# An attention stage and the three dense layers behind it written as one program, with buffers placed by hand

## The chip, the core and the metric

The kernel runs on one core of one Trainium2 chip. Its time is the device time of one launch in microseconds; the medians below are over three runs, and one further execution was taken with the hardware profiler. The engines are called TensorE (PE in the rows; PEld is its weight load), VectorE (DVE), ScalarE (ACT), GpSimd (POOL) and the sync queue (SP).

## The reference

A token matrix `x` of 2048 rows by 512 goes through four residual blocks, all in float32, with inner products kept near float32 accuracy:

```
x = x + attention0(layernorm(x), ctx)     # 16 heads of 128, keys of 128 rows, q and k RMS-normalised
x = x + ffn0(layernorm(x))                # relu(x W1 + b1), relu(. W2 + b2), . W3 + b3 ; 512-1024-1024-512
x = x + attention1(layernorm(x), ctx)     # 32 heads of 16, rotary positions
x = x + experts_and_mlp(layernorm(x))     # gated MLP 2048 wide and a product-key expert lookup
```

The change concerns the first two: in `attention0` every tile of 128 rows attends to its own 128 context rows, heads 0 to 7 and 8 to 15 being independent until their outputs are added.

## The kernel before

Each block is a stage with its own semaphores and its own buffers; `stage_ends()` clears the semaphores and makes all engines wait for one another, and the next stage starts from nothing. Data go between stages through `x1`, `x2`, `x3` in HBM. Within a stage each engine has a list of instructions written out by hand, and semaphores order them across engines; there is no planner.

A float32 product is made of three: each operand is split into a high part (ScalarE, an activation `Copy` that rounds) and a low part (a subtraction, raw minus high), and `product` (L37) adds high by high, high by low and low by high.

`l0_attention` runs 32 steps: steps 0 to 15 do heads 0 to 7 for the 16 row tiles, steps 16 to 31 do heads 8 to 15. Step `s` holds the keys, queries, scores and softmax of tile `s` and, woven in, the end of tile `s-1` (`output`, `turn_p`, `mix`); step 32 is the drain, with only that end. Steps 3 to 13 and 18 to 29 are loops, all others are written out. A step splits its heads in two groups `g` of four. `xres` keeps all rows; `add_y` adds a tile's output there, and `store` writes it to `x1` in the second half. The weights of the first half of the heads are loaded at the start; those of the second half go to `stage` buffers, and around steps 15 and 16 are split into the homes of the first: high parts by ScalarE (L164), low parts by GpSimd (`split_lo(pool, ..., 1)`, L168). In the first half the layer norm's statistics are made on VectorE (L558, L559) and their root on GpSimd (`root`, L274 and L276). `statistics(0)` waits for three loads of `x`, though it reads the first only.

`l0_ffn` runs four chunks of 512 rows. Per chunk: 8 tiles of the first hidden layer (`hidden1`, 12 matmuls each), 8 of the second (`hidden2`, 24 each), and behind each of these a share of the output (`output`, 12 matmuls), with the next chunk's rows normalised, transposed (`turn_x`, L817) and split between. A hidden tile leaves its bank through ScalarE's relu for the high part (L880) and VectorE's relu and subtraction for the low (L938, L941); three banks take turns. Weights come as 16 pieces of 1024 elements a partition through two `stage` buffers: GpSimd fetches and makes the low parts (L799), ScalarE the high ones (L886), in the order W1, W2, W3. The layer norm is wholly on VectorE, its root by ten small instructions (L44 to L48). `hidden2`'s first tile waits for all eight low parts of the first layer.

Of the kernel before, what the change touches and what calls it, by code (L numbers as in the profile page):

```python
# [22 lines left out]
AHEAD = (slice(0, 2), slice(2, NB))  # L23

# [42 lines left out]
def l0_attention(nc, sb, sem, bank, ident, ident_in, x, ctxT, wq, wk, wv, wo, gq, gk, x1):  # L67
# [6 lines left out]


# [58 lines left out]
    LAST_USE = {"wq0": "q_made0", "wq1": "q_made1", "wk0": "k_made0", "wk1": "k_made1", "wv0": "v_made0", "wv1": "v_made1",  # L134
# [25 lines left out]
    def split_hi(act, n, h):  # L160
        act.wait_ge(S[f"{load_of(n)}_staged"], 16 * (h + 1))
        if h:
            act.wait_ge(*at(LAST_USE[n], NB - 1))
        act.activation(home(n, 0), staged(n, h), ACT.Copy).then_inc(S[f"{n}_hi"], 1)  # L164
# [11 lines left out]
    FIRST, LOOP0, END0, LOOP1, END1, LAST = -1, 3, NB - 2, NB + 2, STEPS - 2, STEPS + 1  # L176
# [13 lines left out]
    block = nc.Block()  # L190
    with block:
        @block.sync
        def _(sp):
            x_tiles = x.rearrange("(b p) d -> p b d", p=P)

            def load_res(i):
                tiles = PIECES_OF_X[i]
                sp.dma_start(xres[:, tiles, :], x_tiles[:, tiles, :]).then_inc(S[f"xres_loaded{i}"], 16)

            def load_x(s):  # L200
                row = sp.snap((s - NB) * P)
                if not (isinstance(s, int) and s == NB):
                    sp.wait_ge(*at("xn_ready", s - 1))
                sp.dma_start(x_in[:], x[bass.ds(row, P), :]).then_inc(S["x_loaded"], 16)

            def load_ctx(s):
                if there(s - 1):
                    sp.wait_ge(*at("ctx_split", s - 1))
                row = sp.snap(((s + NB) % NB) * P)
                sp.dma_start(ctx_in[:], ctxT[:, :, bass.ds(row, P)]).then_inc(S["ctx_loaded"], 16)  # L210

            def store(s):
                row, col = sp.snap((s - NB) * P), sp.snap((s - NB) * DM)
                sp.wait_ge(S["y_added"], s + 1)
                sp.dma_start(x1[bass.ds(row, P), :], xres[:].rearrange("p b d -> p (b d)")[:, bass.ds(col, DM)]).then_inc(S["stored"], 16)

            def step(s, second_half=True, storing=True):
                now = s if isinstance(s, int) else None
                if now == FIRST:
                    load_res(0)  # L220
                    load_ctx(0)
                    sp.dma_start(ident[:], ident_in).then_inc(S["ident_loaded"], 16)
                    load_res(1)
                    sp.dma_start(gqk[:, 0:1], gq).then_inc(S["g_loaded"], 16)
                    sp.dma_start(gqk[:, 1:2], gk).then_inc(S["g_loaded"], 16)
                    load_res(2)
                if second_half and there(s + 2):
                    load_x(s + 2)
                if storing:
                    store(s - 1)  # L230
                if there(s + 2):
                    load_ctx(s + 2)
                if now == 0:
                    for i, n in ((3, "wq1"), (4, "wo0"), (5, "wo1")):
                        sp.wait_ge(S[f"{n}_cut"], 1)
                        load_res(i)

            for s in range(FIRST, LOOP0):
                step(s, second_half=False, storing=False)
            with sp.Fori(LOOP0, END0) as s:  # L240
                step(s, second_half=False, storing=False)
            for s in range(END0, LOOP1):
                step(s, storing=s > NB)
            with sp.Fori(LOOP1, END1) as s:
                step(s)
            for s in range(END1, LAST):
                step(s)
            sp.wait_ge(S["stored"], 16 * NB)

        @block.gpsimd  # L250
        def _(pool):
            def fetch(n, h, after=()):
                q, k, v, o = (w[h].rearrange("(k p) w -> p k w", p=P) for w in (wq, wk, wv, wo))
                src = {"wq0": q[:, :, 0:G * D], "wq1": q[:, :, G * D:W], "wv": v, "wk": k, "wo0": o[:, 0:G], "wo1": o[:, G:2 * G]}[n]
                for piece, times in after:
                    pool.wait_ge(S[f"{piece}_cut"], times)
                pool.dma_start(LANDS[h][n].rearrange("p (k w) -> p k w", k=src.shape[1]), src).then_inc(S[f"{n}_staged"], 16)

            def split_ctx(s):
                pool.wait_ge(*at("ctx_hi", s))  # L260
                pool.tensor_tensor(ctxp[1][:], ctx_in[:], ctxp[0][:], ALU.subtract).then_inc(S["ctx_split"], 1)
# [16 lines left out]
            def step(s, roots=False):  # L278
                now = s if isinstance(s, int) else None
                if now == FIRST:  # L280
                    for n in ("wq0", "wk", "wq1", "wv", "wo0", "wo1"):
                        fetch(n, 0)
# [6 lines left out]
                if there(s):  # L289
                    means(s, 0)  # L290
# [1839 lines left out]
```

## Time and profile before

| | us |
|---|---|
| median of three runs | 2245.89 (2243.17 to 2246.0) |
| profiled execution | 2240.67 |
| its span, first to last instruction | 2238.1 |
| first matmul | 21.91 |
| last matmul of `attention0` ends | 787.95 |
| first matmul of `ffn0`'s hidden layer | 821.69 |
| last matmul of `ffn0` ends | 1199.2 |

The span is what the rows divide; the profiled execution's own time is 2.6 us longer. A row of the timeline is start, duration, engine, line, output and inputs; in brackets stands how long the engine had been idle and what released it. The granted clock is TensorE's: 1.0 is 2.4 GHz, 0.5 is 1.2 GHz.

### The profile page before, as it was taken

To read this page: it belongs to the slowest core of one execution; us is meant where nothing else is said; L and a number is where in the kernel's file an instruction comes from. 1 tells how busy PE (TensorE), PEld (TensorE's weight loads), DVE (VectorE), ACT (ScalarE), POOL (GpSimd) and SP (SyncE) were. 2 spreads that over 40 slices of the span, in tenths; PEclk is the share of its full clock that TensorE was granted. 3 is DMA by queue.
4 is the path that set the end of the run, shared out by engine and by line. 5 is a ranking of instruction groups with operands and counts; after the bars stand their busy time and mean duration, and the time that the engine had idled before them with its cause. 6 is when DMAs were issued, how large, how long until landed. Compare 5 with 4: busy or idle time off the path is not lost. (4 is left out here: it accounts for less than half of the span.)

```text
span 2238.1 us, 34003 instructions
## 1 busy us (share of the span) xinstructions
PE 2024.3 (90%) x12656; PEld 1658.0 (74%) x12656; DVE 1344.2 (60%) x2457; ACT 796.5 (36%) x2370; POOL 573.7 (26%) x497
## 2 busy tenths in 40 slices
PE   5999999899999948999994599999559999999998
PEld 4888888788888736787873477777447788778787
DVE  5555555555555556345332667676466778877887
ACT  5555555555555422111110345554223222222121
POOL 3222223512222144000002222332211133333332
PEclk9999999999999969999997699999779999999999
DMA  5100000100000042101013100000211345555445
GB/s 193 65 7 5 5 7 26 65 28 26 30 28 28 12 132 76 39 19 52 5 38 131 42 18 14 21 21 19 68 56 57 113 147 177 183 169 188 168 155 192
DMA packets 77192, 158.13 MB, mean 71 GB/s; under 512 B 8768, under 2 KB 30016, under 8 KB 77120
## 3 DMA queue, kind: packets, MB, share of 16 engines
q0 software_dynamic: 24816, 91.24, 12.2%
q1 hardware_dynamic: 52304, 65.97, 8.9%
q8 instruction: 40, 0.66, 0.1%
q14 instruction: 32, 0.26, 0.0%
HBM read 140.41 MB, written 16.78 MB: 70 GB/s over the span
## 5 line engine op out<-in xcount | busy, mean ns | idle before, releaser
L37 PE MATMUL four_banks<-xT_all,m_w_hi 128*128 (+1 forms) x1024 | 321.2, 395 | 1.1 <-PEq L1558 1.1
L37 PEld LDWEIGHTS four_banks<-xT_all,m_w_hi 128*128 128x128 f32 x1024 | 192.2, 188 | 46.7 <-issue 1.2
L1904 POOL DMA_INDIRECT ring<-in_table,x_row x128 | 123.2, 962 | 325.2 <-DVE y_all L2004 278.6
L37 PE MATMUL four_banks<-xT_all,m_w_lo 128*128 (+1 forms) x512 | 202.3, 395 | 0.0
L938 DVE TENSOR_SCALAR f_relu<-bank,f_b 128x512 f32<-128x512 f32 x64 | 47.9, 749 | 172.0 <-ACT f_h_hi L880 171.8
L480 ACT ACTIVATE prob<-four_banks,mx,rms 128x128 f32<-128x128 f32 x256 | 114.0, 463 | 90.4 <-DVE mx L599 90.4
L880 ACT ACTIVATE f_h_hi<-bank,f_b 128x512 fp32r<-128x512 f32 x64 | 44.0, 688 | 266.7 <-PE bank L37 266.7
L1994 DVE SCALAR_TENSOR_TENSOR x_junk<-x_in,y_ln,ring 128x512 bf16<-128x512 f32 x128 | 126.3, 1020 | 9.9 <-DMA ring<-in_table,x_row 8.7
L267 POOL TENSOR_TENSOR rms<-ssq,constants 128x8 f32<-128x8 f32 x64 | 12.9, 201 | 442.9 <-ACT junk L465 248.3
L37 PE MATMUL bank<-f_h_hi,f_w_hi 128*128 128x512 f32 x256 | 101.8, 398 | 19.3 <-DVE f_h_lo L941 16.2
L1472 DVE TENSOR_REDUCE l_roped<-four_banks 128x16 f32<-128x2048 f32 x32 | 73.4, 2293 | 76.1 <-PE four_banks L1211 76.1
L37 PEld LDWEIGHTS four_banks<-xT_all,m_w_lo 128*128 128x128 f32 x512 | 96.1, 188 | 23.1
L37 PE MATMUL bank<-m_w_hi,m_prod_hi 128*128 128x512 f32 x256 | 101.3, 396 | 11.2 <-DVE m_prod_lo L1936 6.4
L1881 ACT ACTIVATE x_act_of<-x_dot,y_ln 128x2 f32<-128x2 f32 x64 | 18.9, 296 | 258.4 <-DVE x_junk L1994 256.3
L37 PE MATMUL four_banks<-wo_hi,oT_hi 128*128 128x512 f32 x256 | 106.9, 418 | 2.9 <-DVE oT_lo L614 2.8
L269 POOL TENSOR_TENSOR rms<-rms,constants 128x8 f32<-128x8 f32 x64 | 105.1, 1642 | 5.0
L37 PE MATMUL four_banks<-wo_hi,oT_lo 128*128 128x512 f32 x256 | 101.3, 396 | 0.0
L37 PE MATMUL four_banks<-wo_lo,oT_hi 128*128 128x512 f32 x256 | 100.9, 394 | 0.0
L37 PE MATMUL bank<-m_w_lo,m_prod_hi 128*128 128x512 f32 x256 | 100.5, 393 | 0.0
L37 PE MATMUL bank<-m_w_hi,m_prod_lo 128*128 128x512 f32 x256 | 100.5, 393 | 0.0
L37 PE MATMUL bank<-f_h_hi,f_w_lo 128*128 128x512 f32 x256 | 100.3, 392 | 0.0
L37 PE MATMUL bank<-f_h_lo,f_w_hi 128*128 128x512 f32 x256 | 100.2, 391 | 0.0
(295 smaller groups left out, 5401.7 us busy)
## 6 DMA issues: line engine op xcount, KB each, us to landing
f_stage<-in_w POOLq DMA_DIRECT2D x16, 512.0 KB, 4.5
ctx_in<-in_ctxT SPq DMA_DIRECT2D x32, 128.0 KB, 2.5
x_in<-in_x SPq DMA_DIRECT2D x16, 256.0 KB, 2.6
x<-xres SPq DMA_DIRECT2D x16, 256.0 KB, 2.0
f_x_in<-x SPq DMA_DIRECT2D x16, 256.0 KB, 2.7
f_res<-x SPq DMA_DIRECT2D x16, 256.0 KB, 2.8
x<-f_res SPq DMA_DIRECT2D x16, 256.0 KB, 2.1
x<-l_res SPq DMA_DIRECT2D x16, 256.0 KB, 2.1
```

The source lines that it names most:

```text
L37: mm = pe.matmul(out, st, mv, start=first and n == 0, stop=last and n == len(terms) - 1)
L267: pool.tensor_tensor(r[:, 1, :], both, constants[:, 0, :], ALU.add).then_inc(S[f"eps_added{g}"], 1)
L269: pool.tensor_tensor(r[:, 0, :], r[:, 1, :], constants[:, 1, :], ALU.pow).then_inc(S[f"rms_ready{g}"], 1)
L480: a = act.activation(prob[g][:, j, :], bank[(1, 3)[g]][:, j * P:(j + 1) * P], ACT.Exp, bias=mx[g][:, 1, j:j + 1], scale=rms[g][:, 0, j:j + 1],
L880: act.activation(out, bank[HB[(layer * KH + m) % 3]][:], ACT.Relu, bias=b12[:, layer, m:m + 1]).then_inc(S["h_hi"], 1)
L938: dve.tensor_scalar(relu[m % 2][:], bank[HB[(layer * KH + m) % 3]][:], b12[:, layer, m:m + 1], 0.0, ALU.add, ALU.max).then_inc(S["relu_rea ...
L1472: dve.tensor_reduce(m, score_banks.rearrange("p (j t k) -> p j t k", j=4, t=4), AX.X, ALU.max).then_inc(S[f"maxed{f}"], 1)
L1881: act.activation(act_of[:, t, k.start:k.stop], dot[:, t, k.start:k.stop], ACT.Silu, scale=ln[:, t, 1:2]).then_inc(S["silued"], 1)
L1904: pool.indirect_dma_start(ring[:, slot, :], None, table, bass.IndirectOffsetOnAxis(ap=row[:, tile_of(g), k:k + 1], axis=0)).then_inc(S[f"g ...
L1994: d = dve.scalar_tensor_tensor(junk[:, k % PER, :], x_in[t % 2][:], ln[:, t, 0:1], ring[:, slot, 0:DM], ALU.subtract, ALU.mult, accum_out= ...
```

## The change

The two stages become functions that return one program per engine, and each engine runs the attention's and then the dense layers' without a barrier between. Buffers of both are placed at fixed offsets so that the dense layers' early ones lie on attention buffers that are free by then (W1, its stages and rows over the first tiles of `xres`); semaphores of the attention guard the overlaps. The remaining edits:

- Steps 24 to 31 are written out instead of steps 30 and 31 only. In them: two weight loads (step 24, sync queue), high and low parts of W1's four pieces (steps 25 to 28, ScalarE and GpSimd, each followed by GpSimd's next fetch), row loads and bias loads (28), statistics (29), normalisation (30), transposes and splits of the first chunk's four row tiles (31), two more high parts (31), and in the drain three `hidden1` tiles.
- Low parts of the second half's weights: `wk0`, `wk1`, `wq1`, `wv1`, `wo0`, `wo1` go from GpSimd to VectorE; `wq0` and `wv0` stay.
- `statistics(0)` waits for the first load of `x` only, tiles 1 and 2 for theirs.
- Dense layers: weights in the order W1, then two pieces of W2 and one of W3 in turn; W2 and W3 in separate tensors per piece; two banks for hidden tiles instead of three; `hidden2`'s first tile waits for the first layer's low parts one by one; the root of the layer norm on GpSimd; rows of the next chunk in pairs, at `m` of 2 and 6.

```diff
@@ l0_attention
-    FIRST, LOOP0, END0, LOOP1, END1, LAST = -1, 3, NB - 2, NB + 2, STEPS - 2, STEPS + 1
+    FIRST, LOOP0, END0, LOOP1, END1, LAST = -1, 3, NB - 2, NB + 2, AHEAD_FROM, STEPS + 1     # AHEAD_FROM = 24
...
# GpSimd
+            if now is not None and AHEAD_FROM < now < STEPS:
+                ahead["gpsimd"](pool, now)
-                if now == NB:
-                    split_lo(pool, "wv1", 1)
+            if now == STEPS - 1:
+                ahead["root"](pool, 0, 3)
-                    split_lo(pool, "wk0", 1)
-                    split_lo(pool, "wk1", 1)
-                    split_lo(pool, "wq1", 1)
-                if now == NB:
-                    split_lo(pool, "wo0", 1)
-                    split_lo(pool, "wo1", 1)
...
# TensorE, step 31 (STEPS - 1) and drain (STEPS)
+            if now == STEPS - 1:
+                ahead["turn_x"](pe, 0, 0)
             if there(s - 1):
                 output(s - 1, 0)
+                if now == STEPS:
+                    ahead["hidden1"](pe, 0, 0)
                 turn_p(s - 1, 1)
...
+            if now == STEPS:
+                ahead["hidden1"](pe, 0, 1)
             if there(s - 1):
                 mix(s - 1, 1)
+            if now == STEPS - 1:
+                ahead["turn_x"](pe, 0, 1)
...
+            if now == STEPS:
+                ahead["hidden1"](pe, 0, 2)
             if there(s - 1):
                 output(s - 1, 1)
...                                             # turn_x(0, 2) behind values(31, 1), turn_x(0, 3) behind mix(31, 0)
# ScalarE
+            if now is not None and AHEAD_FROM < now <= AHEAD_FROM + 4:
+                ahead["split_hi"](act, now - AHEAD_FROM - 1)
...
+            if now == STEPS - 1:
+                ahead["split_x_hi"](act, 0, 3)
+                ahead["split_hi"](act, 5)
...
# VectorE
-                    for i in (0, 1, 2) if s == 0 else (3, 4, 5) if s == 4 else ():
+                    for i in {0: (0,), 1: (1,), 2: (2,), 4: (3, 4, 5)}.get(s, ()):
+            if now == NB:
+                split_lo(dve, "wq1", 1)
+            if now == NB + 1:
+                split_lo(dve, "wo1", 1)
             if there(s - 1):
                 normalise(s - 1, 1)
                 copy_pT(s - 1, 1)
+            if now == STEPS - 3:
+                ahead["statistics"](dve, 0, 0)
+                ahead["statistics"](dve, 0, 1)
+            if now == STEPS - 2:
+                ahead["layer_norm"](dve, 0, 0)
+                ahead["layer_norm"](dve, 0, 1)
...
                 maxima(s, 0)
+            if now == NB - 1:
+                split_lo(dve, "wk0", 1)
+                split_lo(dve, "wk1", 1)
+            if now in (0, NB):
+                split_lo(dve, "wo0", now // NB)
...
@@ l0_ffn
-    HB = (4, 5, 6)
+    HB = (4, 5)
+    def loads_ahead(sp, s):
+        if s == AHEAD_FROM:
+            sp.wait_ge(A["stored"], 16 * 8)
+            fetch(sp, 0)
+            fetch(sp, 1)
+        if s == AHEAD_FROM + 4:
+            sp.wait_ge(A["stored"], 16 * 12)
+            load_x(sp, 0, 0)
+            load_x(sp, 0, 1)
...
+        if s == 2 * NB - 1:
+            load_x(sp, 0, 2)
+            load_x(sp, 0, 3)
+    def gpsimd_ahead(pool, s):
...
+        if s <= AHEAD_FROM + 4:
+            i = s - AHEAD_FROM - 1
+            split_lo(pool, i)
+            fetch(pool, i + 2)
...
+        def hidden2(c, m, first):
...
+            for k in range(KH):
+                if m == 0:
+                    pe.wait_ge(S["h_lo"], hid(c, 0, k))
...
+        SLOTS = {(0, 4): (6,), (0, 5): (7,), (0, 7): (8,), (1, 0): (9,), (1, 1): (10,), (1, 2): (11,), (1, 3): (12,),
+                 (1, 4): (13,), (1, 5): (14, 15)}      # after which hidden tile ScalarE makes which high part
```

## Rows read from the trace of the kernel before

**Rows 1.** The page: busy time by engine, and granted clock in 40 slices.
```profile
PE 2024.3 (90%) x12656; PEld 1658.0 (74%) x12656; DVE 1344.2 (60%) x2457; ACT 796.5 (36%) x2370; POOL 573.7 (26%) x497
...
PEclk9999999999999969999997699999779999999999
```
**Rows 2.** TensorE by stretch: length, busy (instructions), granted clock, DMA share, GB/s.
```profile
761.00:787.95 26.95, 21.81 (x120) 1.00 0.03 10
787.95:821.69 33.74, 4.38 (x16) 0.54 0.51 166
821.69:845.14 23.45, 23.44 (x96) 0.94 0.34 103
845.14:855.99 10.85, 0.00 (x1) 0.66 0.43 136
855.99:1199.20 343.21, 334.73 (x1488) 1.00 0.10 31
```
**Rows 3.** TensorE's waits up to 1200 us: total, times, longest.
```profile
PE bank L817 <- DVE f_xT_lo L930: 17.3, 3, 7.9
PE bank L37 <- DVE f_h_lo L941: 16.2, 3, 10.8
```
**Rows 4.** DMA issues of the first microseconds: size, us from issue to landing.
```profile
xres<-in_x SPq DMA_DIRECT2D x1, 256.0 KB, 2.7
...
stage<-in_wv POOLq DMA_DIRECT2D x1, 1024.0 KB, 16.9
```
**Rows 5.** Timeline of the start, all engines.
```profile
3.74 0.72 POOL L257 DMA_DIRECT2D stage<-in_wv  x1
...
10.00 1.91 ACT L164 ACTIVATE wq_hi<-stage 128x2048 fp32r<-128x2048 f32 x1 [5.71 <-DMA stage<-in_wq]
18.67 0.69 DVE L558 BATCH_NORM_STATS2 bn<-xres 128x6 f32<-128x512 f32 x1 [18.67 <-DMA xres<-in_x]
...
22.62 2.26 DVE L168 TENSOR_TENSOR wq_lo<-stage,wq_hi 128x2048 fp32r<-128x2048 f32 x1
...
30.40 0.69 DVE L582 COPY q_sb<-bank 128x512 f32<-128x512 f32 x1 [0.45 <-PE bank L37]
```
**Rows 6.** Timeline of TensorE: first matmul of steps 15, 16, 17, 18, 19.
```profile
376.52 0.47 PE L37 MATMUL bank<-wk_hi,ctx_hi 128*128 128x512 f32 x1
...
399.67 0.47 PE L37 MATMUL bank<-wk_hi,ctx_hi 128*128 128x512 f32 x1
...
425.08 0.47 PE L37 MATMUL bank<-wk_hi,ctx_hi 128*128 128x512 f32 x1
...
454.57 0.47 PE L37 MATMUL bank<-wk_hi,ctx_hi 128*128 128x512 f32 x1
...
477.75 0.47 PE L37 MATMUL bank<-wk_hi,ctx_hi 128*128 128x512 f32 x1
```
**Rows 7.** Timeline of VectorE in steps 16 and 17.
```profile
402.83 0.18 DVE L604 RECIPROCAL den<-den 128x4 f32<-128x4 f32 x1 [1.55 <-ACT prob L480]
403.04 3.42 DVE L605 TENSOR_TENSOR prob<-prob,den 128x512 f32<-128x512 f32 x1
...
425.15 4.58 DVE L572 COPY ln_now<-ln 128x2 f32<-128x2 f32 x1
```
**Rows 8.** GpSimd's largest group, 400 to 431 us: count, busy, mean ns, idle.
```profile
L168 POOL TENSOR_TENSOR wo_lo<-stage,wo_hi 128x2048 fp32r<-128x2048 f32 x2 | 9.1, 4564 | 0.0
```
**Rows 9.** Groups of the dense layers' weight splits, 790 to 900 us.
```profile
L799 POOL TENSOR_TENSOR f_w_lo<-f_stage,f_w_hi 128x1024 fp32r<-128x1024 f32 x16 | 38.6, 2413 | 35.7 <-ACT f_w_hi L886 35.6
...
L886 ACT ACTIVATE f_w_hi<-f_stage 128x1024 fp32r<-128x1024 f32 x16 | 16.9, 1055 | 36.7 <-DMA f_stage<-in_w 20.0 <-DMA f_b<-in_b 16.7
```
**Rows 10.** Timeline of TensorE in the drain.
```profile
778.05 0.50 PE L37 MATMUL four_banks<-wo_hi,oT_hi 128*128 128x512 f32 x1 [1.41 <-DVE oT_lo L614]
```
**Rows 11.** Timeline of VectorE and TensorE at the second chunk's layer change.
```profile
946.19 0.74 DVE L938 TENSOR_SCALAR f_relu<-bank,f_b 128x512 f32<-128x512 f32 x1
...
949.18 0.49 PE L37 MATMUL bank<-f_h_hi,f_w_hi 128*128 128x512 f32 x1 [2.59 <-DVE f_h_lo L941]
```

More of the change, by code:

```diff
@@ L23, with spots_of @@
 AHEAD = (slice(0, 2), slice(2, NB))
+AHEAD_FROM = 24
+def spots_of(start, text):
+    words = text.split()
+    out, at = {}, int(1024 * start)
+    for name, kb in zip(words[::2], words[1::2]):
+        out[name] = at
+        at += int(1024 * float(kb))
+    return out
 def part_products(parts_a, parts_b):
@@ new lines, in sync, with load_res, store, finish @@
+    def sync(sp):
+        def load_res(c, j, first):
+            row = sp.snap((c * TPC + j) * P)
+            if not (first and j < 2):
+                sp.wait_ge(S[f"stored{j % 2}"], 16 * (2 * c + j // 2))
+            sp.dma_start(res[j % 2][:], x1[bass.ds(row, P), :]).then_inc(S[f"res_loaded{j % 2}"], 16)
+        def store(c, j):
+            row = sp.snap((c * TPC + j) * P)
+            sp.wait_ge(S["y_added"], tile_of(c, j))
+            sp.dma_start(x2[bass.ds(row, P), :], res[j % 2][:]).then_inc(S[f"stored{j % 2}"], 16)
+        def finish(c, first=False):
+            for j in range(TPC):
+                store(c, j)
+                if j + 2 < TPC:
+                    load_res(c, j + 2, first)
+        def step(c, first=False, last=False):
+            load_res(c, 0, first)
+            load_res(c, 1, first)
+            if not last:
+                for j in range(TPC):
+                    load_x(sp, c + 1, j)
+            finish(c, first)
+        sp.wait_ge(A["stored"], 16 * NB)
+        sp.dma_start(b3r[:], b3).then_inc(S["b3_loaded"], 16)
+        step(0, first=True)
+        with sp.Fori(1, NC - 1) as c:
+            step(c)
+        step(NC - 1, last=True)
+        for i in range(2):
+            sp.wait_ge(S[f"stored{i}"], 16 * 2 * NC)
@@ new lines, in gpsimd, with add_bias, step @@
+    def gpsimd(pool):
+        def add_bias(c, j):
+            pool.wait_ge(S[f"res_loaded{j % 2}"], 16 * (2 * c + j // 2 + 1))
+            pool.tensor_tensor(res[j % 2][:], res[j % 2][:], b3r[:], ALU.add).then_inc(S["bias_added"], 1)
+        def step(c, first=False, last=False):
+            if not first:
+                add_bias(c - 1, 2)
+                add_bias(c - 1, 3)
+            add_bias(c, 0)
+            add_bias(c, 1)
+            if not last and not first:
+                for j in range(TPC):
+                    root(pool, c + 1, j)
+        for i in range(4, len(ORDER)):
+            if i in (9, 13):
+                root(pool, 1, (i - 9) // 2)
+                root(pool, 1, (i - 9) // 2 + 1)
+            split_lo(pool, i)
+            if i + 2 < len(ORDER):
+                fetch(pool, i + 2)
+        pool.wait_ge(S["b3_loaded"], 16)
+        step(0, first=True)
+        with pool.Fori(1, NC - 1) as c:
+            step(c)
+        step(NC - 1, last=True)
+        add_bias(NC - 1, 2)
+        add_bias(NC - 1, 3)
```

1394 lines of the change are left out of this document (721 added, 673 removed).

## The prediction

> **What bounds the kernel now.** I read the page first. TensorE is busy for 90% of the span and no other engine comes near it; only its idle stretches and its half-speed stretches (1.2 GHz against 2.4 GHz, granted clock 0.5 against 1.0) can be won back [rows 1, 2]. So I cut TensorE's time by stretches, and then asked the waits which instruction ended each gap [rows 2, 3]. The reader is to see three places, all in the stages that the change rewrites. In the drain of the attention TensorE is busy for 21.81 of 26.95 us: 5.14 idle. In the join it is busy for 4.38 of 33.74 us, with a mean granted clock of 0.54. In the dense layers it then runs 96 matmuls, stands 10.85 us, and runs 343.21 us with 8.45 us of short gaps (343.21 less 334.73). The waits name the joins' enders: normalised rows, transposes and their splits, and for 16.2 us in three gaps the low part of a hidden tile. Two smaller places follow from the timeline: the start, in which the first matmul waits for data [rows 4], and two long steps at the exchange of the weight halves [rows 5, 6].
>
> **Start.** The change lets the first statistics wait for the first row tile alone. Now they start at 18.67 us, when all of three pieces are there, though the first piece, issued within the first microsecond, landed 2.7 us later [rows 4]. VectorE then splits `wq0` at 22.62 and copies the first queries at 30.40 [rows 5]. In the new order the first statistics come at about 4 us, the second, for a second piece of the same size, before `wq0` can be split, `wq0`'s high part is ready at 10.00 + 1.91 = 11.9, its low part 2.3 us later at 14.3, the first transpose's (0.7) at 15.0 [rows 5]. The first product takes as long as now, some 4.9 us, so queries could be copied at 20. But VectorE does the low parts of `wk0`, `wk1` and `wq1` before that, and `wq1` lands between `wq0` (10.0) and `wv` (3.74 + 16.9 = 20.6) [rows 4, 5]. With 17 as an estimate for it: high part 18.9, low part 21.2, queries copied at 21.2 instead of 30.40: 9.2 us gained. The ends: it lands by 15.8 (gain 10.4), or with `wv` at 20.6 (gain 5.6). The `wv` parts are then no limit: loaded 20.6, both high parts 22.6, low parts 24, against 34.2 now.
>
> **Exchange of halves.** Step 16 takes 425.08 − 399.67 = 25.41 us and step 17 takes 29.49; a looped one (step 18) 477.75 − 454.57 = 23.18 and an unrolled one (step 15) 23.15 [rows 6]. The excess is 2.2 + 6.3 = 8.5 us. Its cause: a VectorE multiply of 512 elements took 3.42 us and a copy of two elements 4.58 us [rows 7], both while GpSimd was in a 2048-element subtraction of 4.56 us [rows 8]. A VectorE subtraction of four times as many elements takes 2.26 [rows 5]; the multiply and the copy were held, and ended only when GpSimd had. The change hands six of these subtractions to VectorE: 2.3 us for each 2048-element one. `wq1` and `wo1` go between the split of the mixed output and the normalisation, where VectorE now idles 1.55 us for ScalarE's exponentials [rows 7], `wo0` goes behind the maxima, `wk` and `wv1` into further idle places. I count 0.7 us of overrun at the two places where 2.3 meets 1.55, mostly under TensorE's queue: 0.6 us left, 7.9 gained. The ends: 5 (each of the three large ones shows its overrun) and 8.5.
>
> **Steps 24 to 31 of the attention.** Two loads of weights, four splits and four more fetches, two row loads with two bias loads, and the rows' statistics are added. Unrolling six more steps costs nothing by the two steps without additions above [rows 6]. The sync queue waits for eight stored tiles (about 2 us behind the store) before it issues the context load, but that load waits for a split 5 us later anyway. ScalarE's four high parts (1.06 us each) and GpSimd's four low parts (2.4 us each) [rows 9] lie in idle stretches of both, and what VectorE then does reads PSUM, unlike the held instructions of rows 7. Statistics (2 × 0.9 us in step 29) and normalisation (2 × 0.55 in step 30) end before TensorE wants the keys. I take 0; the ends are 0 (nothing here can gain) and 4 × 2.4 = 10 us, should every split hold a VectorE instruction that TensorE waits for.
>
> **Drain and join.** Now the last step's first output begins at 778.05 behind 1.41 us of idle [rows 10], and the last matmul ends at 787.95 [rows 2]. In the new order it begins later, by these terms: two row transposes ahead of the values, 0.43 each, 0.9; ScalarE's row split (0.6) and one more transpose in front of the copies that TensorE needs, with what VectorE has to do beside them, 1.0; the transpose of the last rows 0.4, and behind it ScalarE's row split (0.6) and a whole weight split (1.0) queued in front of its own of the mixed output, of which 1.55 shows. That is 3.9. To it come 2.0: GpSimd starts its 2.4 us subtraction for the fifth piece just as VectorE is to normalise, and by rows 7 and 8 VectorE is held to its end. Rows two and three load while the step runs: the turning of rows zero and one frees their buffers 13 us before the new rows are turned. So 778.05 + 3.9 + 2.0 = 783.95. From there TensorE has 6.8 us of its own (24 matmuls of 0.23, a transpose group, a mix) and three hidden tiles of 2.73 = 8.2 us, which now fill the gaps whole: the attention ends at 798.95, and three of the dense layers' tiles are done by then. Taken as one unbroken stretch those layers begin at 798.95 − 8.2 = 790.75 instead of 821.69: 30.9 us gained. Ends: 28 (the held instruction twice and a late row) and 33.
>
> At this place the Trainium skill has a rule. "GPSIMD Engine Reference", section Key points, says that GpSimd contends with VectorE instructions in a 2-port mode or with two SBUF inputs. By it the held multiply and copy of rows 7 are to be expected, readers of PSUM are spared, and the 2.0 us stand; without the rule the time would be 2 us less.
>
> **Dense layers.** What is left of the 10.85 + 8.45 = 19.3 us of gaps: the new second-layer product waits for the first layer's tiles one by one, and its first seven take 4.8 us, more than the 2.6 that the last tile's two parts need, so the 10.85 and the 2.6 to 3.1 at each of three chunks go. The two stretches at 1.2 GHz go too: 96 matmuls took 23.44 us where 0.228 each makes 21.9 (334.73 us less 5.2 for twelve transpose groups, over 1440 matmuls, gives 0.229) [rows 2], so 1.5 us, and about 1.3 behind the 10.85 us gap. New is that only two banks hold hidden tiles: the product after next waits for VectorE's relu. The tight place: relu starts at 946.19 and ends 946.93, while TensorE is ready at 949.18 − 2.59 = 946.59 [rows 11]; 0.35 us at each of three chunks. In the first chunk the single pair of stages paces sixteen pieces: each needs some 5 us of load, 1.06 and 2.4 [rows 9]; TensorE wants the last of them 74 us after the join, and by the written slots I find each ready 5 us or more before. 1 us is set aside there for relu delayed by GpSimd. So 19.3 + 2.8 − 1.05 − 1 = 20.1 us gained. Its ends: 9 (the weights make the first chunk wait as now) and 22.
>
> **Sum.** 9.2 + 7.9 + 0 + 30.9 + 20.1 = 68.1 us. The profiled execution took 2240.67 us (span 2238.1), so 2172.6; it lies 5.2 under the median of the three runs, 2245.89, from which I count: 2177.8 us. Later stages are untouched: their own long gap begins after a barrier that stays.
>
> **Rivals.**
> 1. The preparation disturbs the attention. For: GpSimd and VectorE do hold one another up [rows 7, 8], and four splits, 1.06 and 2.36 us each, are added to steps that run without any gap now. Against: the places are idle. Price 10 us, time 2188. Chance 0.12.
> 2. The first dense chunk waits for weights. For: it is what ScalarE's waits produced before, and two stages serve sixteen pieces. Against: six pieces are in before the chunk begins. Price 11 us, time 2189. Chance 0.10.
> 3. The change doesn't do what it says at the join: rows two and three can be loaded only when rows zero and one are turned, so the gap of 33.7 us stays in part, 10 to 20 us behind the values. Against: 13 us lie between first turning and first use. Time about 2192. Chance 0.05.
> 4. Slower than before: TensorE loses its clock. The change joins stretches into one of some 1100 us almost without a gap; the longest run without a low digit is now fourteen slices (780 us), and the gap of step 17 lies in it [rows 1]. If the granted clock fell to 0.5 in the attention, each matmul would cost 0.43 instead of 0.23; of each 0.43 us so spent 0.20 are lost, so the gain of 68 us is used up from 68 × 0.43 / 0.20 = 146 us at 1.2 GHz, and 160 such us would make 2252. For it speaks only that no row shows such a length; against it, that every half-speed stretch here follows an idle stretch. Chance 0.02.
> 5. More than forecast, `wq1` early and no drain penalty: 2172. Chance 0.13, inside the range.
>
> **How the numbers follow.** The forecast has the remaining 0.58. Its own range is 2170 to 2186. To it the bounds add: gains of 5.6 to 10.4, 5 to 8.5, −10 to 0, 28 to 33 and 9 to 22; they will not all fall on one side, and 2168 to 2196 leaves out less than 2 in 10. About 0.2% (4.5 us) is what a measurement can tell here from no change. Every case but the fourth is faster by more: 0.97 faster, 0.01 the same, 0.02 slower.
>
> **What would show it.** First query copy near 21 us. Steps 16 and 17 at 23.2 to 24 us, no VectorE instruction over 3 us in them. Steps 25 to 30 still 23.17. In the drain, one TensorE gap near 3 us before the last step's first output, none over 1 us until the second layer; granted clock 1.0 from the exchange through the dense layers. No wait of TensorE for the low hidden tile over 1 us. Wrong would be: a step 25 to 28 above 24 us, a wait in the first dense chunk for a weight's low part, a VectorE multiply held in a step where I count none, or a second gap at 1.2 GHz.

## The result and the profile after

The changed kernel took **2180.83 us**, the median of 4 runs (2176.76 to 2182.68), beside 2244.53 us for the kernel before (4 runs, 2240.41 to 2246.0). The ratio is 0.9717, with a 95% interval from 0.9697 to 0.9736. The forecast was 2177.8 us. Measured again later, the same kernel took 2176.59 us (5 runs) against 2244.8 (9 runs): ratio 0.9699, 0.9675 to 0.9722.

The page of the changed kernel, against [rows 1]: busy time by engine and the granted clock by slice.
```profile
span 2178.5 us, 33626 instructions
...
PE 2020.0 (93%) x12656; PEld 1656.1 (76%) x12656; DVE 1308.4 (60%) x2287; ACT 795.8 (37%) x2370; POOL 564.1 (26%) x523
...
PEclk9999999999999999999995899999689999999999
```
TensorE runs as many matmuls as before and the span is 59.6 us shorter. The low digit at the join (slice 15 of before) is gone; those of slices 22, 23, 29 and 30 belong to the later stages, which aren't changed, and are still there (with other digits).

TensorE by stretch, against [rows 2]: the drain with its last part of step 31; the hundred microseconds behind it; the stretch in which all of the dense layers' TensorE work would fit, its first 8.2 us reckoned back from 789.29 for the three tiles made earlier.
```profile
745.87:789.29 43.42, 34.99 (x170) 0.88 0.12 37
789.29:889.24 99.95, 99.95 (x449) 1.00 0.23 73
781.10:1138.00 356.90, 355.38 (x1589) 1.00 0.13 42
```
The join with its 33.74 us at a clock of 0.54 does not exist any more, and the dense layers stand still for 1.5 us in all. What is left is idle time inside the drain: 43.42 less 34.99.

TensorE's waits from 736 to 1140 us, against [rows 3]: total, times, longest.
```profile
PE four_banks L48 <- DVE oT_lo L660: 4.7, 1, 4.7
PE four_banks L340 <- DVE prob L651: 2.0, 1, 2.0
PE bank L48 <- DVE f_relu L1100: 1.5, 4, 0.5
PE four_banks L395 <- DVE kT_sb L639: 1.1, 1, 1.1
PE four_banks L340 <- ACT prob L511: 0.7, 1, 0.7
```
There is no wait for a low hidden tile, for a weight's low part or for a row's part. The four waits of the drain sum to 8.4 us, which is all of that idle time; the forecast had one of about 3.

I cut both profiled executions at the same instructions: first matmul of steps 1, 18 and 31, the last matmul of the dense layers, the end. "Dense end" is reckoned from the start of step 31, so that it holds the drain, the join and the dense layers, in whatever order their work is done; "attention end" is part of it. All in us.

| | to step 1 | steps 1-17 | 18-30 | 31 to attention end | 31 to dense end | after | span |
|---|---|---|---|---|---|---|---|
| before | 51.24 | 403.33 | 301.26 | 32.09 | 443.34 | 1038.93 | 2238.1 |
| changed | 44.46 | 394.98 | 301.26 | 48.75 | 397.35 | 1040.45 | 2178.5 |
| gain | 6.8 | 8.35 | 0 | | 46.0 | -1.5 | 59.6 |
| forecast | 9.2 | 7.9 | 0 | | 30.9 + 20.1 | 0 | 68.1 |

The profiled executions are 2240.67 and 2180.29 us, 60.4 apart; the medians of the two kernels 63.7. The sum of my terms was 7.7 too high, yet the forecast median came within 3.0 us, because that profile of before lay 5.2 below its median while the changed kernel's lies 0.5 below its own. That part of the agreement is luck.

### The profile page after: what moved, and what is told of

It reads as the page before. It is cut to its first block and busy times, and to the rows that moved or that the text cites. A ratio compares the mean times of both kernels' runs of the same rounds, so it can differ in the third digit from the quotient of the medians.

```text
span 2178.5 us, 33626 instructions
## 1 busy us (share of the span) xinstructions
PE 2020.0 (93%) x12656; PEld 1656.1 (76%) x12656; DVE 1308.4 (60%) x2287; ACT 795.8 (37%) x2370; POOL 564.1 (26%) x523
## 5 line engine op out<-in xcount | busy, mean ns | idle before, releaser
L2158 DVE SCALAR_TENSOR_TENSOR x_junk<-x_in,y_ln,ring 128x512 bf16<-128x512 f32 x128 | 119.4, 967 | 9.7 <-DMA ring<-in_table,x_row 8.5
```

What stands on the lines that cost most here:

```text
L2158: d = dve.scalar_tensor_tensor(junk[:, k % PER, :], x_in[t % 2][:], ln[:, t, 0:1], ring[:, slot, 0:DM], ALU.subtract, ALU.mult, accum_out= ...
```

## The experiments

Ten altered kernels and the changed one again, each profiled; `again` and `d_all` were executed five times each, the others once. `d_lo4`, `d_hi5`, `d_hi5_lo4` and `d_fill` ran on one chip, where the kernel before took 2237.63 us; the other seven ran on another, where it took 2246.78 and 2244.8. The same sections of each (us):

| | to step 1 | 1-17 | 18-30 | 31 to attention end | 31 to dense end | after | span |
|---|---|---|---|---|---|---|---|
| b_start_exch | 43.02 | 394.90 | 301.26 | 32.03 | 441.90 | 1043.52 | 2224.6 |
| u_ahead | 41.95 | 394.90 | 301.26 | 33.61 | 418.43 | 1045.96 | 2202.5 |
| u_h1 | 40.99 | 395.20 | 301.25 | 45.49 | 402.25 | 1043.01 | 2182.7 |
| u_h2 | 43.21 | 394.96 | 300.99 | 49.64 | 408.93 | 1037.31 | 2185.4 |
| again | 41.79 | 395.17 | 300.99 | 48.68 | 397.25 | 1039.60 | 2174.8 |
| d_lo4 | 42.31 | 394.98 | 301.25 | 46.61 | 395.45 | 1036.11 | 2170.1 |
| d_hi5 | 46.37 | 394.98 | 301.26 | 47.08 | 396.06 | 1042.13 | 2180.8 |
| d_hi5_lo4 | 44.49 | 394.91 | 301.25 | 44.21 | 392.53 | 1042.32 | 2175.5 |
| d_fill | 44.28 | 394.95 | 301.25 | 46.41 | 395.14 | 1044.08 | 2179.7 |
| d_all | 45.21 | 395.20 | 301.26 | 41.27 | 389.98 | 1041.65 | 2173.3 |
| f_start | 45.23 | 394.93 | 301.25 | 48.08 | 396.87 | 1047.62 | 2185.9 |

Read the columns downward first. Steps 1 to 17 and 18 to 30 agree within 0.3 us in all runs that share their code. The start, with the same code in ten of the eleven, spreads over 5.4 us (40.99 to 46.37), and the last part, with the same code in all, over 11.5 us (1036.1 to 1047.6). One total can't tell two microseconds of the drain apart; a section can, within its own spread: four executions have the changed kernel's drain, and from the start of step 31 to the attention's end they took 48.08 (`f_start`), 48.68, 48.75 and 49.64 us (`u_h2`). Their idle times before each instruction are the same within 0.4 us; what differs is where the clock fell.

**The small edits alone.** `b_start_exch` is the kernel before with the start's and the exchange's edits.
```diff
-                    for i in (0, 1, 2) if s == 0 else (3, 4, 5) if s == 4 else ():
+                    for i in {0: (0,), 1: (1,), 2: (2,), 4: (3, 4, 5)}.get(s, ()):
...
-                    split_lo(pool, "wo0", 1)
-                    split_lo(pool, "wo1", 1)
...
+                if now == NB:
+                    split_lo(dve, "wq1", 1)
+                if now == NB + 1:
+                    split_lo(dve, "wo1", 1)
```


> The kernel before with two parts of the change alone: the first statistics wait for the first load only, and six low parts at the exchange of halves go from GpSimd to VectorE. Theory A (both parts act by themselves): step 1 begins 6.8 us earlier than before (44.46 against 51.24), step 18 another 8.4 earlier (439.4), the dense layers are untouched, span 15.1 us shorter: 2223. Rival B (the hand-placed buffers or the common program have a share in it): one of the two differences is smaller by over 0.5 us.

Measured: 8.2 us at the start, 403.33 − 394.90 = 8.43 us in steps 1 to 17, 1.4 in the drain and the dense layers, sum 13.5 of span with 4.6 lost in the last part. The start's 8.2 lies beside 6.8 in the changed kernel, inside the 5.4 us by which the start varies; both edits give their gain without the join's.

**The preparation taken out of the attention.** One program, no barrier between, but everything for the dense layers is issued behind the attention.
```diff
-                programs0["gpsimd"](pool, ahead)
+                programs0["gpsimd"](pool, nothing)
+                for s in range(25, 32):
+                    ahead["gpsimd"](pool, s)
+                ahead["root"](pool, 0, 3)
...
+                for j in range(4):
+                    ahead["turn_x"](pe, 0, j)
+                for m in range(3):
+                    ahead["hidden1"](pe, 0, m)
```


> One program without a barrier, but all the preparation (weights, rows, statistics, transposes, the three hidden tiles) is issued only behind the attention's last instruction of each engine. Theory A (the preparation is the larger part of the join's gain, the missing barrier the smaller): the join keeps a gap of about 20 us between the attention's last matmul and the first hidden one (33.7 before, less 4.2 for the barrier and 8 for the shorter roots), the drain has its 5 us of idle back, and the span is 20 to 26 us over the changed kernel's 2178.5. Rival B (the barrier and the serial roots were the cost): span no more than 8 us over it.

Measured: 2204.29 us. TensorE from the start of step 31, by stretch, in `u_ahead`:
```profile
738.11:771.72 33.61, 28.47 (x145) 0.95 0.02 9
771.72:797.85 26.13, 4.47 (x18) 0.55 0.61 193
797.85:1156.54 358.69, 357.09 (x1584) 1.00 0.13 42
```
The join is back with 26.13 us against 33.74 before, where I had expected about 20; the drain has its 5.1 us of idle again (33.61 less 28.47), and the span is 24.0 over the changed kernel's, of which 21.1 lie in this section. From step 31 to the dense layers' end it takes 418.43 us: 24.9 less than before, 21.1 more than the changed kernel. So doing the work early is worth 21.1 us. The 24.9 are a join 7.6 shorter without the barrier, dense layers 18.8 shorter by their new order (358.69 against 377.48), and 1.5 lost in the drain.

**The early hidden tiles taken out alone.**
```diff
-                if now == STEPS:
-                    ahead["hidden1"](pe, 0, 0)
...
-    BEGUN = 3
+    BEGUN = 0
```
(and so for the other two tiles, with their rounding and relu.)

> The three hidden tiles are taken out of the drain and made behind it; the preparation of weights and rows stays. Theory: the tiles fill the gaps in which TensorE waits for the weighted values' parts, turned values and copies, so without them their 8.2 us come back behind the attention's end less what little they delay it: from step 31's start to the point at which three hidden tiles and the attention are done (48.75 us in the changed kernel) 52 to 57 us, so 3 to 8 us lost. Rival: the tiles only move work and fill nothing, because the waits they cover are set by ScalarE and VectorE whose queues they lengthen: 48 to 50 us.

Measured: the attention ends 48.75 − 45.49 = 3.26 us earlier after the start of step 31, and the dense layers 4.9 us later (402.25 against 397.35). TensorE's work in three tiles is 8.2 us; it lengthens the drain by only 3.3. TensorE in that stretch of `u_h1`, to be laid beside the changed kernel's 48.75 us with 40.32 busy (below):
```profile
737.44:782.93 45.49, 35.32 (x162) 0.81 0.14 41
```
The idle time is 10.17 us without the tiles and 8.43 with them, so they fill only 1.7 us of gaps. The other 3.2 us are clock: 36 more matmuls add 5.0 us of busy time and not 8.2, since the mean granted clock rises from 0.81 to 0.89. Of the 21.1 us of the early work, 4.9 are thus the tiles, and by difference 16.2 the rows and weights that are ready.

**The new order of the second layer undone.** Its first tile waits for the low part of all hidden tiles.
```diff
+            if m == 0:
+                pe.wait_ge(S["h_lo"], hid(c, 0, KH - 1))
             for k in range(KH):
-                if m == 0:
-                    pe.wait_ge(S["h_lo"], hid(c, 0, k))
```


> The changed kernel, but the second layer's first tile waits for all eight low parts of the first layer again. Theory A: a gap of 2.6 us at each of the four chunks comes back, in place of the 0.3 to 0.4 us waits for the relu: 9 to 9.5 us more, no change of the granted clock. Rival B: the gaps before were due to the biases' additions on VectorE and do not come back whole: under 5 us.

TensorE's waits of `u_h2` from 736 to 1140 us:
```profile
PE bank L48 <- DVE f_h_lo L1103: 9.8, 4, 2.6
...
PE bank L48 <- DVE f_relu L1100: 0.6, 1, 0.6
```
Measured: four gaps of 2.32 to 2.57 us, and the dense layers end 11.6 us later (408.93 against 397.35), of which 0.9 lies in the drain, whose code is the same. The remaining 10.7 are somewhat more than the 9 to 9.5 expected. 9.8 are the waits, less 0.9 of relu waits that they hide. The rest, nearly 2, is TensorE's busy time for the same 1548 matmuls (348.83 us against 347.07); part of it is seen in the last chunk, where twelve matmuls behind the gap took 4.00 us at a mean clock of 0.65.

**The four gaps of the drain.** TensorE in the changed kernel (start, duration; in brackets the idle time before and its releaser), against [rows 10]:
```profile
758.52 0.63 PE L340 MATMUL four_banks<-ident,k_sb 128*128 128x128 f32 x4 [0.72 <-ACT prob L511]
761.12 0.66 PE L340 MATMUL four_banks<-ident,prob 128*128 128x128 f32 x4 [1.98 <-DVE prob L651]
762.84 1.56 PE L395 MATMUL four_banks<-kT_sb,qT_sb 128*128 128x128 f32 x8 [1.06 <-DVE kT_sb L639]
771.64 0.79 PE L48 MATMUL four_banks<-wo_hi,oT_hi 128*128 128x512 f32 x1 [4.67 <-DVE oT_lo L660]
```
VectorE of the same stretch:
```profile
758.62 2.45 DVE L651 TENSOR_TENSOR prob<-prob,den 128x512 f32<-128x512 f32 x1
...
768.95 2.03 DVE L645 SCALAR_TENSOR_TENSOR mx<-mx,rms 128x4 f32<-128x4 f32 x1
770.91 0.68 DVE L660 TENSOR_TENSOR oT_lo<-four_banks,oT_hi 128x512 fp32r<-128x512 f32 x1
```
GpSimd and ScalarE:
```profile
758.17 2.35 POOL L856 TENSOR_TENSOR f_w_lo<-f_stage,f_w_hi 128x1024 fp32r<-128x1024 f32 x1
...
768.63 2.33 POOL L856 TENSOR_TENSOR f_w_lo<-f_stage,f_w_hi 128x1024 fp32r<-128x1024 f32 x1 [7.05 <-ACT f_w_hi L852]
```
```profile
767.00 0.60 ACT L1035 ACTIVATE f_xT_hi<-bank 128x512 fp32r<-128x512 f32 x1 [7.16 <-PE bank L974]
767.50 1.05 ACT L852 ACTIVATE f_w_hi<-f_stage 128x1024 fp32r<-128x1024 f32 x1
768.44 0.59 ACT L518 ACTIVATE oT_hi<-four_banks 128x512 fp32r<-128x512 f32 x1
```
Two things are to be seen. GpSimd's first subtraction runs from 758.17 to 760.52, and VectorE's multiply of two SBUF operands, which started inside it, took 2.45 us instead of 0.69: it ends 0.55 us behind the subtraction. GpSimd's second runs from 768.63 to 770.96, and VectorE's scaling of four maxima, 0.16 us otherwise, takes 2.03 and ends 0.02 us behind it; `oT_lo`, for which TensorE waits, is queued behind it. The second subtraction starts then because ScalarE has just rounded the sixth weight piece, ahead of `oT_hi`. The Trainium skill's "GPSIMD Engine Reference", Key points, has the contention with VectorE instructions of two SBUF inputs; this trace agrees, and shows it for an instruction of four elements per partition.

Edits: `d_lo4` lets GpSimd wait for the normalised rows before its fifth subtraction; `d_hi5` moves ScalarE's sixth rounding behind the exponentials of the drain; `d_hi5_lo4` does both; `d_fill` puts the first hidden tile ahead of the last step's first output; `d_all` has all three.
```diff
+        pool.wait_ge(S["xn_ready"], 4)
         for i in range(4, len(ORDER)):
```
```diff
                 ahead["split_x_hi"](act, 0, 3)
-                ahead["split_hi"](act, 5)
...
             if now == STEPS:
+                ahead["split_hi"](act, 5)
                 ahead["hidden_hi"](act, 0, 0, 0)
```
```diff
+            if now == STEPS:
+                ahead["hidden1"](pe, 0, 0)
             if there(s - 1):
                 output(s - 1, 0)
-                if now == STEPS:
-                    ahead["hidden1"](pe, 0, 0)
```


> GpSimd waits for the fourth normalised row tile before it makes the low part of the fifth weight piece; nothing else. Theory A (its subtraction holds VectorE's multiply of two SBUF inputs): the multiply of 2.45 us takes 0.69, TensorE's gap of 1.98 us before the transposed probabilities goes to 0.2 or less, and the 1.06 us gap behind it shrinks too, 2.5 to 3 us in all. Rival B (the gap comes from ScalarE's longer queue in step 31, and the multiply is late anyway): the gap stays over 1.2 us. The 4.67 us gap before the drain's first output stays under both.

> ScalarE's high part of the sixth weight piece is moved from the end of step 31 to behind the exponentials of the drain; nothing else. Theory A (the split in ScalarE's queue costs 1.0 us, and the GpSimd subtraction that it sets off holds a small two-input VectorE instruction for 1.9 us, both in front of the drain's first output): TensorE's gap there falls from 4.67 to about 1.8 us, and the small instruction takes 0.16 us again. Rival B (only ScalarE's queue matters): the gap falls by 1.0, to 3.7 us. The hold at the multiply in front of the transposed probabilities (1.98 us) stays under both. Start of the drain's first output 2.9 us earlier under A, 1.0 under B; what the clock does I leave open, since one gap of 2 us stays.

> Both edits together. Theory A with the clock: with two gaps of 2 and 4.7 us gone or nearly gone TensorE stays at 2.4 GHz through the drain, where it now spends 12 output matmuls and some transposes at 1.2 GHz, about 4 us of loss; the dense layers' first whole hidden tile then begins 5.5 + 4 = 9 us earlier than in the changed kernel (789.3 us there). Rival C (the half-speed stretch does not follow from these gaps): the gaps go, the clock still falls, and the gain is 5 us, the sum of the two edits alone.

> The first hidden tile is moved in TensorE's order from behind the drain's first output to before it; nothing else. Theory A (the 4.67 us gap is a wait for VectorE and ScalarE that other matmuls can fill): the tile's rows are ready 1.4 us into the gap, so a gap of some 1.5 us, then 12 matmuls, then the output without a wait: 2.7 to 3.2 us gained at 1.0 clock, and the gap between output and transposed probabilities stays closed. Rival: the hidden tile runs at half speed (12 x 0.43 = 5.1 us), so it overshoots the gap and gains 2 us or less.

> The changed kernel once more, as the yardstick of this chip for the next one. Theory: 2176 to 2183 us, ratio to the kernel before 0.970 to 0.974. From the start of step 31 to the attention's last matmul 48.75 us in its profile before; if the gaps of the drain come from the order of work, the same four are there again (0.72, 1.98, 1.06, 4.67 us). Rival: they are chance of one execution, and the stretch differs by over 1 us.

> All three edits of the drain together: GpSimd's subtraction for the fifth piece waits for the normalised keys of the drain, ScalarE's sixth piece is rounded behind the exponentials, and the first hidden tile stands ahead of the last step's first output. Theory: each removes its own gap. Step 31's start to the attention's last matmul was 48.75 us in the changed kernel and 44.21 us with the first two; what is left there is a gap of 2.81 us, which a hidden tile of 2.8 us fills: 41.5 to 42.5 us, so 6.2 to 7.2 us less than the changed kernel beside it, and the medians differ by 4 to 8 us. Rival: the hidden tile ahead of the output waits itself (1.50 us in the run in which it stood alone, because its rows' parts come behind ScalarE's and VectorE's queues), and the stretch stays at 43.5 to 44.5, the medians 3 to 5 us apart.

`d_lo4`, VectorE: the multiply is free, while the scaling is held as before.
```profile
756.47 0.69 DVE L651 TENSOR_TENSOR prob<-prob,den 128x512 f32<-128x512 f32 x1
...
764.93 2.03 DVE L645 SCALAR_TENSOR_TENSOR mx<-mx,rms 128x4 f32<-128x4 f32 x1
```
`d_hi5`, VectorE: the scaling is free, since the subtraction comes later.
```profile
771.37 0.16 DVE L645 SCALAR_TENSOR_TENSOR mx<-mx,rms 128x4 f32<-128x4 f32 x1
```
`d_hi5_lo4`, TensorE: both are free, and the gap of 4.67 us has become 2.81.
```profile
767.97 0.51 PE L48 MATMUL four_banks<-wo_hi,oT_hi 128*128 128x512 f32 x1 [2.81 <-DVE oT_lo L660]
```
`d_all`, TensorE: the gap has become 1.50.
```profile
759.49 0.63 PE L340 MATMUL four_banks<-ident,k_sb 128*128 128x128 f32 x4 [0.72 <-ACT prob L511]
760.95 0.63 PE L340 MATMUL four_banks<-ident,prob 128*128 128x128 f32 x4 [0.83 <-ACT qT_sb L506]
762.05 2.02 PE L395 MATMUL four_banks<-kT_sb,qT_sb 128*128 128x128 f32 x8 [0.47 <-DVE kT_sb L639]
767.67 0.47 PE L48 MATMUL bank<-f_xT_hi,f_w_hi 128*128 128x512 f32 x1 [1.50 <-DVE f_xT_lo L1094]
```
From step 31's start to the attention's end: 48.75 in the changed kernel (48.68 in `again`, with the same four gaps), 46.61 in `d_lo4` (2.1 less), 47.08 in `d_hi5` (1.7), 46.41 in `d_fill` (2.3), 44.21 in `d_hi5_lo4` (4.5) and 41.27 in `d_all` (7.5). So both held instructions are shown as causes, each by an edit that frees it and leaves the other held, and the gaps aren't chance: the four executions with this drain all have 1.97 or 1.98 us and 4.67 or 4.68. (`d_hi5` moves ScalarE's rounding too, so its part holds both the freed scaling and an earlier `oT_hi`.) The sizes are less sure, one execution each beside a spread of 1.6 us. Together they bring 4.54 against 2.14 + 1.67; that difference is within the spread.

Several expectations were missed. In `d_lo4` I had expected 2.5 to 3 us and a gap of at most 0.2; the gap is 0.83, behind ScalarE. In `d_hi5` the gap fell from 4.67 to 2.81 and not to 1.8, and the output began 1.36 us earlier in its step and not 2.9, because TensorE ran longer at 1.2 GHz before it. In `d_hi5_lo4` I had expected 9 us if the clock stayed up; it didn't, and the 4.5 us are nearer to the rival's 5. `d_fill`'s 2.3 lie between the 2.7 of the theory and the 2 of its rival.

By stretch from the start of step 31 to the attention's end, in the changed kernel, `d_hi5`, `d_lo4`, `d_hi5_lo4` and `d_all`:
```profile
740.70:789.45 48.75, 40.32 (x198) 0.89 0.12 38
```
```profile
742.61:789.69 47.08, 40.75 (x198) 0.86 0.13 40
```
```profile
738.54:785.15 46.61, 39.91 (x198) 0.89 0.12 40
```
```profile
740.65:784.86 44.21, 39.37 (x198) 0.92 0.13 42
```
```profile
741.67:782.94 41.27, 37.74 (x198) 0.96 0.15 45
```
The number of matmuls is the same; the busy time falls from 40.32 to 37.74 as the mean clock rises from 0.89 to 0.96. Of the 7.5 us of `d_all`, 4.9 are gaps and 2.6 matmuls that ran at 2.4 instead of 1.2 GHz.

The drain has a second stretch at 1.2 GHz, in front of the gap of 4.67 us, in the scores and values. In the changed kernel it follows the gaps of 0.72, 1.98 and 1.06 us; `d_all` still has it, behind gaps of 0.72, 0.83 and 0.47 us. The changed kernel, then `d_all`:
```profile
763.50:766.60 3.10, 3.10 (x17) 0.50 0.26 100
```
```profile
762.40:765.50 3.10, 3.10 (x16) 0.50 0.00 0
```
It costs some 1.5 us, half of the 3.10. The kernel before had its gaps of 1.16, 0.34 and 1.41 us in this place and kept a granted clock of 1.00. What sets it off is not shown.

In time, with 5 rounds: `d_all` 2174.08 us (2167.63 to 2175.14), ratio to before 0.9674 (0.966 to 0.9689), beside 2176.59 and 0.9699 (0.9675 to 0.9722) for `again` on the same chip. The intervals overlap: 2.5 us between the medians is less than I expected from 7.4 us in the section, and whether the whole is faster is not shown. In the profiled pair 3.4 us went at the start and 2.1 in the last part, where both kernels have the same code.

**The start.** Idle transposes (24 before the first queries, 20 before the first turning) were to keep the clock up.
```diff
+            if isinstance(s, int) and s == 0 and g == 0:
+                busy(24)
...
+            if now == FIRST:
+                busy(20)
```


> The changed kernel with 24 idle transposes of the identity put in front of the first queries and 20 behind them, written to a bank not yet in use; their results are never read. Theory A (the start lost 1.5 us of its 8.3 because TensorE's gaps of 5.2 and 2.9 us keep it at 1.2 GHz up to about 33 us): the first queries take 2.8 us instead of 5, the transposes and keys behind 22.8 us run at full speed, step 1 begins 1.4 us earlier, 43.0. Queries ready earlier gain nothing themselves, since their copy on VectorE waits for the third weight's low part. Rival B (the lost 1.5 us sit in other waits): step 1 begins at 44.4 as now.

Measured: no gain; step 1 begins at 45.23 against 44.46, with the first queries copied 0.8 us later because data landed later in that run. The first queries did run at full speed, as expected, but a gap of 2.69 us stayed behind them, and from there to step 1 it took 21.66 us, as in the changed kernel. So the loss lies behind this gap and not in front of it. A comparison of runs with the same code shows the same. TensorE from 23 to 45 us in the changed kernel, in `again` and in `d_hi5`:
```profile
23.00:45.00 22.00, 20.21 (x108) 0.93 0.23 82
```
```profile
23.00:45.00 22.00, 19.50 (x111) 1.00 0.38 138
```
```profile
23.00:45.00 22.00, 19.75 (x93) 0.85 0.17 57
```
The turning of the first queries followed gaps of 2.90, 1.51 and 3.16 us, and from there to step 1 it took 21.65, 20.13 and 22.91 us; 31.14 to 51.24, 20.10 us, before. The shorter gap left the clock at 1.0, the longer ones were followed by a mean of 0.93 and 0.85. All other executions fall in line: behind gaps of 0.79 to 1.99 us (`u_h1`, `d_lo4`, `u_ahead`, `b_start_exch`) it took 20.1 us, behind 2.14 to 2.89 us (`d_fill`, `u_h2`, `d_hi5_lo4`, `d_all`) 21.7 to 22.9. That holds for this place; in the drain shorter gaps were enough.

## Why the forecast came out as it did

**Start: direction right, 9.2 forecast, 6.8 measured.** VectorE in the changed kernel, against [rows 5]:
```profile
3.55 0.69 DVE L604 BATCH_NORM_STATS2 bn<-xres 128x6 f32<-128x512 f32 x1 [3.55 <-DMA xres<-in_x]
...
11.87 2.29 DVE L190 TENSOR_TENSOR wq_lo<-stage,wq_hi 128x2048 fp32r<-128x2048 f32 x1 [0.54 <-ACT wq_hi L186]
...
19.86 2.29 DVE L190 TENSOR_TENSOR wq_lo<-xres,wq_hi 128x2048 fp32r<-128x2048 f32 x1 [2.68 <-ACT wq_hi L186]
22.07 0.69 DVE L628 COPY q_sb<-bank 128x512 f32<-128x512 f32 x1
```
The chain is the one I wrote down: statistics at 3.55 (about 4), `wq0`'s low part ready at 14.1 (14.3), `wq1`'s at 22.1 (21.2), queries copied at 22.07 instead of 21.2: 8.3 us gained, 0.9 short because of `wq1`'s landing, for which I only had an estimate. The other 1.5 us are the half-speed matmuls behind the 2.90 us gap, a term that I left out. By the eleven executions with this code (step 1 at 40.99 to 46.37, against the one profile of before) it is worth 4.9 to 10.3 us, where my ends were 5.6 and 10.4; one profile says little of its middle.

**Exchange of halves: 7.9 forecast, 8.35 measured, 8.43 alone.** No VectorE instruction in these steps is over 2.35 us, where 3.42 and 4.58 stood in [rows 7]; the 2048-element subtractions take 2.29:
```profile
408.26 2.29 DVE L190 TENSOR_TENSOR wo_lo<-stage,wo_hi 128x2048 fp32r<-128x2048 f32 x1
...
417.71 2.28 DVE L190 TENSOR_TENSOR wo_lo<-stage,wo_hi 128x2048 fp32r<-128x2048 f32 x1
```
The overrun of 0.6 us that I had set aside isn't there: steps 16 and 17 take 23.26 and 23.25 us.

**Steps 18 to 30: 0 forecast, 0 measured**, to 0.01 us. Rival 1 is out: four splits by GpSimd beside TensorE's steps held nothing that it waited for.

**Drain and join: 30.9 forecast, 25.5 measured.** (443.34 − 397.35 = 46.0, less 20.5 for the dense layers, below.) This is the step that was mis-sized: 25.5 lies outside its own ends of 28 and 33. The lower one did allow for "the held instruction twice". "So 778.05 + 3.9 + 2.0 = 783.95" puts the last step's first output 28.12 us behind the start of step 31; it came 771.64 − 740.70 = 30.94 behind it, 2.8 late. Before, it was 22.22, so the two terms of 2.0 and 3.9 measured 8.7. `d_hi5_lo4`, with both instructions free and the sixth rounding moved, has it at 767.97 − 740.65 = 27.32 and splits the 8.7: 3.6 for the held instructions with that rounding, and 5.1 for the rest. I had counted one held instruction, at 2.0 us; there are two, and the second is one that I would not have looked at, four elements long. It follows from what I wrote of ScalarE: I had the sixth rounding in front of the mixed output's, and didn't ask what GpSimd would do with it. The rest is over its 3.9 by 1.2 or more, about what the stretch at 1.2 GHz in the scores and values costs (1.5, above); I had put no clock into this term. The other 2.8 us lie behind the output: "From there TensorE has 6.8 us of its own" was at full speed, and I had written "granted clock 1.0". But the gap of 4.67 us was followed by twelve matmuls at 1.2 GHz, in the changed kernel:
```profile
771.64:776.90 5.26, 5.26 (x12) 0.50 0.33 100
776.90:789.30 12.40, 12.40 (x62) 0.99 0.00 0
```
Twelve matmuls in 5.26 us where 12 × 0.23 = 2.8 would do: 2.5 of the 2.8 us. By my own signs this was wrong in three points: the clock was to stay at 1.0, no gap but one was to be over 1 us, and there was to be no second gap at 1.2 GHz. Three edits of the order win the 5.6 us back, and more: `d_all`'s attention ends 41.27 us after step 31's start, 1.9 before my 43.1. Freeing the two held instructions alone isn't enough (`d_hi5_lo4`: 44.21, 1.1 behind it); the rest comes with the hidden tile in front of the output. That the idea of the join was right is shown by `u_ahead`: 21.1 us come back when the work isn't done early. The rivals for this part fell: no wait for weights in the first dense chunk (2), none for rows (3).

**Dense layers: 20.1 forecast, 20.5 measured.** Before, 1199.17 − 821.69 = 377.48 us; after, 1138.05 − (789.29 − 8.2) = 356.95. Relu waits are 1.5 us in all, in four places, where I had set 1.05 for three and 1 for GpSimd. GpSimd does hold VectorE in the first chunk, but under TensorE's queue:
```profile
801.16 0.75 DVE L1100 TENSOR_SCALAR f_relu<-bank,f_b 128x512 f32<-128x512 f32 x1 [1.15 <-ACT f_h_hi L1047]
801.95 1.72 DVE L1103 TENSOR_TENSOR f_h_lo<-f_relu,f_h_hi 128x512 fp32r<-128x512 f32 x1
...
810.77 2.62 DVE L1087 TENSOR_SCALAR f_x_in<-f_x_in,f_mv 128x512 f32<-128x512 f32 x1
```
**The clock (rival 4).** TensorE of the changed kernel in the attention, almost without a gap:
```profile
46.00:757.00 711.00, 710.30 (x4044) 1.00 0.11 34
```
711 us in one go, and 356.9 in the dense layers, kept a granted clock of 1.00; the rival is out. **More than forecast (rival 5)** did not come in the changed kernel; `d_lo4`, at 2171.93 in one execution, reached it by an early start and a short last part as much as by its 2 us, and on a chip where the kernel before took 2237.63.

**Left open:** why the last part (the same code in all) takes 1036.1 us in one execution and 1046.0 or more in another. TensorE's busy time in it goes from 909.7 to 916.7 us with a mean clock of 0.94 and 0.93 (`d_lo4`, `u_ahead`), so longer matmuls, at a lower mean clock, are 7 of the 10 us; what makes the difference between executions no run here tells.

## What to carry to other kernels

When work of a next stage is laid into the last steps of this one, cost each inserted instruction with what it sets off on the next engine: here ScalarE's rounding released a GpSimd subtraction, and that one held a VectorE instruction of four elements with two SBUF operands. Put the clock into every term that holds new gaps of TensorE: here the gap of 4.67 us cost another 2.5 behind it, and three gaps of 0.47 to 0.83 us in `d_all` were followed by 3.1 us at 1.2 GHz. And where a program's ends vary by several microseconds from execution to execution, compare stretches between the same two instructions, not totals, and measure how far such a stretch varies by itself.

## What the runs showed of the hardware that was not expected

- How long VectorE was held went by what was left of GpSimd's subtraction and not by its own size: 4 elements per partition took 2.03 us (0.16 free), 512 elements 2.45 us (0.69 free). An instruction with one SBUF operand and a scalar (`f_x_in`) was held as well, 2.62 us against 0.53 free. A relu that reads PSUM, begun at 801.16 inside the subtraction of 800.69 to 803.10, took its usual 0.75, and the two-operand one right behind it 1.72.
- A gap of TensorE of 4.67 us was followed by some 5.3 us at a granted clock of 0.50 in the changed kernel. But the clock fell behind much shorter gaps too (3.1 us at 0.50 behind 0.72, 0.83 and 0.47 us in `d_all`), and `d_hi5` and `d_fill`, whose largest gaps are 2.81 and 1.98 us, had a lower mean clock (0.86 and 0.85) over the same stretch than the changed kernel (0.89). So the size of the largest gap doesn't say how much is lost.
- Work put into the drain paid mostly by the clock: three hidden tiles filled 1.7 us of gaps and raised the mean granted clock from 0.81 to 0.89, which gave 3.2 us (`u_h1` against the changed kernel, one execution each).
